# A graph network's segment sums on one core: when VectorE reads the table positions of the gathered groups

## The chip, the cores and the metric

The kernel runs on one core of a Trainium2 chip, as one launch. The metric is the device time of that launch in microseconds (us). A core has five engines that run their own instruction streams and meet at semaphores: TensorE (PE in the profile; PEld is its weight load), VectorE (DVE), ScalarE (ACT), GpSimd (POOL) and SyncE (SP), beside 16 DMA engines. Each engine has a sequencer that reads the stream in order, does register work and waits itself, and hands the rest to the engine. In the profile the sequencer's own instructions carry a q (DVEq).

## The reference, cut to what matters

Two layers of a graph network over 12500 nodes and 200000 edges, with the edges sorted by destination. The first layer is a pair of neighbour sums:

```python
agg = jax.ops.segment_sum(x[src], dst, num_segments=segments)   # 12500 x 32
h = relu(agg @ W_l_in.T + b_l_in + x @ W_r_in.T)
out = segment_sum(h[src], dst) @ W_l_out.T + b_l_out + h @ W_r_out.T
x = layernorm(x + out)
```

The second layer is an attention layer on the same edges (scores per edge, softmax over a destination's edges, a weighted segment sum, a projection and a layernorm). The change touches only the two neighbour sums of the first layer.

## The kernel before, in words

Each neighbour sum is one call of `segment_sum_pass`, the first with the tag sum_x, the second with the tag sum_y. In the trace the first lies between about 80 and 940 us, the second between about 980 and 1730 us. The rest of the span belongs to other functions. A pass adds the rows of the source nodes of 200000 sorted edges into a table in SBUF, `table_a`, which has the nodes along its free axis. It does so in two ways at once.

**The head** is the part of the edges with many edges per destination. It isn't gathered. VectorE makes, for tiles of 128 edges, two small 0/1 matrices: `lows` (line 1054) and `cells` (line 1066, written into the tile e_tab). TensorE multiplies them (line 981), which counts how often each source stands in each destination. ScalarE copies the counts to SBUF (line 949, one eviction for each unit of two PSUM banks). TensorE multiplies a block's counts with the node values (`parts`, line 1006). VectorE reduces the result and makes its places (lines 1090 and 1092), TensorE shifts it into a window of 128 nodes (line 1019), and VectorE adds the window into `table_a` at a position that is data (line 1104). That position is one number, read into a register by the load of line 1095, once for each block. In the first pass SyncE also stores the counts of 48 blocks to DRAM, 3200 KB each (line 901, count_scratch). In the second pass those blocks are loaded instead of counted.

**The tail** is gathered. GpSimd issues indirect DMAs (line 892) that bring 8 tiles of 128 edges for each slot; a slot is two groups of 512 edges, and four slots are in flight (SLOTS = 4). TensorE multiplies a group's rows with a 0/1 matrix (line 1030), made by VectorE in the first pass (`make_onehot`, line 1040) and by ScalarE in the second. VectorE adds the two windows of a slot into `table_a`: one addition for each group in the first pass, on 96 partitions, three in the second, on 32 partitions each (line 1123). The positions of the two groups are data too. They stand in `win`, an int32 row on partition 0 with one number for each group.

**Order.** Everything is written out by hand in steps: `Plan` assigns units, products, window additions and gathered tiles to steps by a table of costs, and each engine's program walks the same steps. VectorE's program makes the cells two steps ahead of their use (LEAD = 2) into a ring of four (RING = 4). In each step it makes cells, then reduces, then adds windows of the head, then makes the next 0/1 matrix of the tail, then adds the tail's windows. The additions of a slot stand one step after its last matrix product.

**The load.** Line 1112 reads positions of `win` into registers of VectorE's sequencer. It stands in front of the additions of every fourth slot, ahead of the wait for the slot's product, and reads the positions of four slots, eight numbers, with one instruction (six for the last three slots of the first pass). In the first pass the first slot is number 129, so the first load begins at number 258 of `win`; in the second it is slot 144, number 288.

```python
if i % SLOTS == 0:
    last = min(G, (n0 + i + SLOTS) * SG)
    starts = nc.values_load_multi_w_load_instructions(
        win[0:1, (n0 + i) * SG:last], engines=DVE_ENGINE, min_val=0, max_val=N,
        skip_runtime_bounds_check_because=CLAMPED)[1]
dve.wait_ge(summed, i + 1)
```

Of the kernel before, what the change touches and what calls it, by code (L numbers as in the profile page):

```python
# [23 lines left out]
DVE_ENGINE = [mybir.EngineType.DVE]  # L24
# [6 lines left out]
WINDOW = 128  # L31
SLOTS = 4
SG = 2
# [15 lines left out]
CLAMPED = "set-up clamps the starts"  # L49
# [206 lines left out]
def build(nc, x, src, dst, edge_attr, wl_in, bl_in, wr_in, wl_out, bl_out, wr_out,  # L256
          w1, b1, w2s, b2s, w2d, b2d, attn, out):
    N, E = x.shape[0], src.shape[0]
    IT, G, J, NCH = sizes(N, E)
# [20 lines left out]
    with ExitStack() as whole:  # L280
# [38 lines left out]
        table_a = sb("table_a", [P, NCH * GROUP])  # L319
# [6 lines left out]
        win = sb("win", [1, G], I32)  # L326
# [9 lines left out]
        at = COUNTS  # L336
        head_key, at = scratch[:, at:at + HT], at + HT
        head_low, at = scratch[:, at:at + HT], at + HT
        spare_at = at
        count_up, at = scratch[:, at:at + WIDEST * NK // 2].bitcast(F16), at + WIDEST * NK // 2  # L340
# [22 lines left out]
        with ExitStack() as ctx:  # L363
# [3 lines left out]
            even, last = FULLJ // 16 * 16, min(96, FULLJ // 32 * 32)  # L367
# [453 lines left out]
        def segment_sum_pass(tag, table_dram, values, plan, store):  # L821
# [14 lines left out]
            with ExitStack() as ctx:  # L836
# [199 lines left out]
                def _(dve):  # L1036
# [34 lines left out]
                    if not read:  # L1071
# [1 line left out]
                        dve.memset(unused[:, :, 56:], 0.0).then_inc(padded, 1)  # L1073
                        dve.tensor_copy(whole_row, iota[:, :]).then_inc(numbered, 1)
                        dve.wait_ge(numbered, 1)
                    made, starts, heads_added, tails_added = plan.first_item, [], 0, 0
                    if not lent:
                        make_onehot(0)
                    for step in range(plan.steps):
                        while made < plan.end_item and head.items[made]["first"] < (  # L1080
                                plan.first_unit + plan.made_by[step + LEAD]):
                            make_cells(made)
                            made += 1
                        for b in plan.parts_at.get(step, ()):
                            j = plan.place[b]
                            dve.wait_ge(multiplied, j + 1)
                            if j >= 2:
                                dve.wait_ge(windowed, j - 1)
                            columns = head.blocks[b]["columns"]
                            dve.tensor_scalar(places[0:columns, j % 2, :], iota[0:columns, :],  # L1090
                                              head_rel[0:columns, b:b + 1], UNPAIR, ALU.is_equal, ALU.mult)
                            dve.tensor_reduce(sums[0:columns, j % 2, :], product_of(j)[0:columns, :]  # L1092
                                              .rearrange("p (w f) -> p f w", w=3), AX.X, ALU.add).then_inc(summed_up, 1)
                        for b in plan.add_at.get(step, ()):
                            first = nc.values_load_multi_w_load_instructions(
                                head_win[0:1, b:b + 1], engines=DVE_ENGINE, min_val=0, max_val=N,
                                skip_runtime_bounds_check_because=CLAMPED)[1][0]
                            dve.wait_ge(windowed, plan.place[b] + 1)
                            if plan.place[b]:
                                dve.wait_ge(head_added, plan.place[b])  # L1100
                            if tails_added:
                                dve.wait_ge(tail_added, tails_added)
                            to = table_a[2 * F:3 * F, bass.ds(first, WINDOW)]
                            dve.tensor_tensor(to, to, window_of(plan.place[b]), ALU.add).then_inc(head_added, 1)
                            heads_added += 1
                        for i, t in taken.get(step, ()):
                            if t == 0 and lent <= i + 1 < slots:
                                make_onehot(i + 1)
                        for i in adds.get(step, ()):
                            if i % SLOTS == 0:  # L1110
                                last = min(G, (n0 + i + SLOTS) * SG)
                                starts = nc.values_load_multi_w_load_instructions(
                                    win[0:1, (n0 + i) * SG:last], engines=DVE_ENGINE, min_val=0, max_val=N,
                                    skip_runtime_bounds_check_because=CLAMPED)[1]
                            dve.wait_ge(summed, i + 1)
                            for g in range(SG):
                                for rows, sums_of in takes:
                                    if tails_added:
                                        dve.wait_ge(tail_added, tails_added)
                                    if heads_added:  # L1120
                                        dve.wait_ge(head_added, heads_added)
                                    to = table_a[rows, bass.ds(starts[i % SLOTS * SG + g], WINDOW)]
                                    dve.tensor_tensor(to, to, slot_sums(i, g)[sums_of, :], ALU.add)\
                                       .then_inc(tail_added, 1)
                                    tails_added += 1
# [1423 lines left out]
```

## Time and profile before

| what | value |
|---|---|
| median of 3 runs | 3997.3 us (3989.62 to 3998.96) |
| the profiled execution | 4001.15 us, its span 3999.3 us |
| PE busy over the span | 2838.4 us, 71% |
| DVE busy | 2714.7 us, 68% |
| ACT busy | 2490.8 us, 62% |
| POOL busy | 2638.2 us, 66% |

The span is the time from the first to the last instruction; 1.85 us of the profiled execution lie outside it. The shares are averages over stages with different limits, so they don't say what bounds a sum pass; that is read stage by stage. In a row that tells what ended an engine's idle time, a name after the arrow is the instruction that released it. "issue" means that the profile shows nothing that the engine waited for: its sequencer was busy with something else or hadn't got there yet.

### The profile page before, as it was taken

What the parts mean: (1) busy time and instruction counts of PE and PEld (TensorE: products, weight loads), DVE (VectorE), ACT (ScalarE), POOL (GpSimd) and SP (SyncE); (2) the same over time, 40 slices, a digit from 0 to 9 for tenths busy, and PEclk for the clock granted to TensorE, in tenths of its full rate; (3) what the DMA queues carried; (4) which work ended last, traced back from release to release, by engine and by line L of the source; (5) the groups of instructions that cost most, each with busy time, mean ns of one, the idle gap of its engine ahead of it and who ended that gap; (6) DMA issues with size and microseconds to landing.
All of it is one profiled execution on the core that took longest, in us unless ns stands there. A gap on an engine that the chain in (4) does not pass through costs nothing. (4 is left out here: it accounts for less than half of the span.)

```text
span 3999.3 us, 82215 instructions
## 1 busy us (share of the span) xinstructions
PE 2838.4 (71%) x28125; PEld 2379.6 (60%) x28125; DVE 2714.7 (68%) x7548; ACT 2490.8 (62%) x7102; POOL 2638.2 (66%) x2669
## 2 busy tenths in 40 slices
PE   3688788887888888874567666676666666667646
PEld 2566566664777777764456655565555665656644
DVE  7898766774455455562467777777876777777776
ACT  4566666775666566630167766787666776677745
POOL 3466765774655565427777777777777777777735
PEclk9999989998999999985567776677776777677767
DMA  3677875113666676723333333333333333333311
GB/s 88 237 284 312 315 313 213 21 20 118 223 232 234 222 237 222 237 92 69 76 77 87 90 85 76 87 94 86 85 82 78 93 87 83 79 82 88 89 31 39
DMA packets 285952, 536.14 MB, mean 134 GB/s; under 512 B 116631, under 2 KB 203217, under 8 KB 278902
## 3 DMA queue, kind: packets, MB, share of 16 engines
q1 hardware_dynamic: 200032, 452.07, 32.7%
q0 software_dynamic: 80256, 76.21, 10.2%
q8 instruction: 229, 3.75, 0.4%
q10 hardware_dynamic: 5246, 2.56, 0.2%
q14 instruction: 189, 1.55, 0.1%
HBM read 355.50 MB, written 175.09 MB: 133 GB/s over the span
## 5 line engine op out<-in xcount | busy, mean ns | idle before, releaser
L2034 POOL DMA_INDIRECT scratch<-fs_scratch,src_idx x728 | 728.8, 1001 | 222.0 <-issue 221.4
L892 POOL DMA_INDIRECT gath<-x_parts,src_idx x532 | 538.8, 1013 | 316.6 <-issue 191.5
L949 ACT ACTIVATE scratch<-sum_x_ps_c 128x600 int32<-128x600 f32 (+5 forms) x690 | 520.0, 770 | 311.2 <-PE sum_x_ps_c L981 266.6
L1066 DVE TENSOR_SCALAR e_tab<-scratch,e_tab 128x700 bf16<-128x700 f16 (+8 forms) x1380 | 526.1, 423 | 257.8 <-PE sum_y_ps_c L981 226.5
L892 POOL DMA_INDIRECT gath<-y_parts,src_idx x412 | 406.6, 987 | 291.6 <-issue 121.0
L2162 ACT ACTIVATE scratch<-scratch,bias,weight 128x32 f32<-128x32 f32 x1360 | 483.7, 399 | 77.2 <-DVE bias L2232 77.2
L2076 PEld LDWEIGHTS ps_e<-fdw,scratch 128*128 128x128 f32 x3136 | 494.3, 239 | 23.2
L2243 DVE SCALAR_TENSOR_TENSOR scratch<-ps_e,attn_sb 128x128 f32<-128x128 f32 x784 | 189.4, 284 | 429.0 <-PE ps_e L2076 427.8
L2076 PE MATMUL ps_e<-fdw,scratch 128*128 128x66 f32 x3136 | 478.0, 319 | 0.0
L949 ACT ACTIVATE scratch<-sum_y_ps_c 128x700 int32<-128x700 f32 (+2 forms) x348 | 280.1, 832 | 279.7 <-PE sum_y_ps_c L981 274.5
L1006 PEld LDWEIGHTS sum_x_ps_d<-parts,scratch 128*128 128x128 f16 x7400 | 383.3, 101 | 102.3 <-ACT scratch L949 44.4
L2142 ACT ACTIVATE scratch<-iota,dst_rel 128x128 f32<-128x128 f32 x824 | 251.2, 387 | 307.3 <-PE ps_m L2096 307.3
L1006 PE MATMUL sum_x_ps_d<-parts,scratch 128*128 128x96 bf16 x7400 | 419.0, 211 | 28.1 <-DVE scratch L1092 16.7
L981 PE MATMUL sum_x_ps_c<-e_tab,onehot 128*128 128x300 bf16 (+5 forms) x1380 | 323.3, 320 | 153.8 <-DVE e_tab L1066 116.2
L2034 POOL DMA_INDIRECT nodes<-fs_scratch,src_idx x332 | 325.7, 981 | 101.3 <-issue 100.9
L2034 POOL DMA_INDIRECT kept_spare<-fs_scratch,src_idx x280 | 274.4, 980 | 85.4 <-issue 85.1
L2096 PE MATMUL ps_m<-scratch 128*64 128x128 f32 x1456 | 266.6, 359 | 20.7 <-DVE scratch L2285 16.5
L2034 POOL DMA_INDIRECT gath<-fs_scratch,src_idx x224 | 225.3, 1006 | 76.4 <-issue 68.0
L1006 PE MATMUL sum_y_ps_d<-parts,scratch 128*128 128x96 bf16 x4500 | 239.8, 212 | 36.8 <-DMA scratch<-count_scratch 21.2
L2070 PE MATMUL ps_e<-scratch,ident 128*128 128x264 f32 x364 | 150.6, 553 | 155.5 <-DMA scratch<-fs_scratch,src_idx 155.4
L2096 PEld LDWEIGHTS ps_m<-scratch 128*64 128x64 f32 x1456 | 238.0, 188 | 31.1 <-DVE scratch L2285 18.1
L1006 PE MATMUL sum_y_ps_c<-parts,scratch 128*128 128x96 bf16 x4500 | 241.2, 213 | 18.9 <-ACT scratch L949 15.2
(363 smaller groups left out, 6241.3 us busy)
## 6 DMA issues: line engine op xcount, KB each, us to landing
count_scratch<-scratch SPq DMA_DIRECT2D x48, 3200.0 KB
scratch<-count_scratch SPq DMA_DIRECT2D x192, 800.0 KB
onehot<-rel_scratch SPq DMA_DIRECT2D x196, 256.0 KB
scratch<-in_edge_attr_2x SPq DMA_DIRECT2D x390, 128.0 KB
fdw<-fd_scratch SPq DMA_DIRECT2D x392, 33.0 KB
scratch<-fs_scratch,src_idx POOLq DMA_INDIRECT x728
gath<-x_parts,src_idx POOLq DMA_INDIRECT x532
gath<-y_parts,src_idx POOLq DMA_INDIRECT x412
```

Source lines behind the costliest of these rows:

```text
L892: pool.indirect_dma_start(out=rows_in(s, t), out_offset=None, in_=table_dram, in_offset=bass.IndirectOffsetOnAxis(ap=src_idx[:, g, k:k + 1 ...
L949: act.activation(to, ps_c[u % pairs][:, :, 0:q].rearrange("p h (d a) -> p h a d", d=d), ACT.Copy).then_inc(kept, 1)
L981: m = pe.matmul(ps_c[u % pairs][:, h, 0:q], lows[:, tile // LOWS % RING, tile % LOWS, :], cells[:, item % RING, at:at + q], start=True, st ...
L1006: m = pe.matmul(product_of(j), counts[:, plan.buffer(b), a, :], parts[:, a, :], start=(a == 0), stop=(a == NK - 1))
L1066: d = dve.tensor_scalar(cells[:, n % RING, i * width:(i + 1) * width], count_up[:, 0:width], head_key[:, tile:tile + 1], head_weight[:, ti ...
L2034: pool.indirect_dma_start(out=rows_of(m)[:, t, :], out_offset=None, in_=fs_dram, in_offset=bass.IndirectOffsetOnAxis(ap=src_idx[:, g, k:k ...
L2070: pe.matmul(ps_e[s % 2][g][:, :, 0:ROW], ident[:, :], rows_of(m)[:, g * K:(g + 1) * K, :], start=True, stop=False)
L2076: t = pe.matmul(ps_e[s % 2][g][:, k, 0:ROW], oht[:, s % 2, g * K + k, :], fdw[:, s, g, :], start=False, stop=(k == K - 1))
L2096: t = pe.matmul(ps_m[par][:, g * WINDOW:(g + 1) * WINDOW], rows_of(n - 2)[:, g * K + k, 0:HID], oh_msg[:, par, g * K + k, :], start=(k == ...
L2142: far = act.activation(to[:, t, :], iota[:, :], ACT.Square, bias=places[:, t:t + 1], scale=-1.0)
L2162: e = act.activation(rows, rows, ACT.Exp, bias=bias[:, q, i:i + 1], scale=weight[:, q, i:i + 1], accum_out=total[:, q, i:i + 1] if i < K * ...
L2243: dve.scalar_tensor_tensor(parts[:, :, h, 0:F], ps_e[s % 2][g][:, :, h * F:(h + 1) * F], 0.0, wide(attn_sb[:, h * F:(h + 1) * F], 1, [P, K ...
```

## The change

The block that loaded eight positions in every fourth slot goes. In its place stand, in every slot, two loads of one position each, for the slot's two groups, at the same place of the program: behind the previous work of VectorE and ahead of the wait for the slot's product. The additions take their position from these two. Nothing else changes.

```diff
-                    made, starts, heads_added, tails_added = plan.first_item, [], 0, 0
+                    made, heads_added, tails_added = plan.first_item, 0, 0
...
                         for i in adds.get(step, ()):
-                            if i % SLOTS == 0:
-                                last = min(G, (n0 + i + SLOTS) * SG)
-                                starts = nc.values_load_multi_w_load_instructions(
-                                    win[0:1, (n0 + i) * SG:last], engines=DVE_ENGINE, min_val=0, max_val=N,
-                                    skip_runtime_bounds_check_because=CLAMPED)[1]
+                            at = (n0 + i) * SG
+                            starts = [nc.values_load_multi_w_load_instructions(
+                                win[0:1, at + g:at + g + 1], engines=DVE_ENGINE, min_val=0, max_val=N,
+                                skip_runtime_bounds_check_because=CLAMPED)[1][0] for g in range(SG)]
                             dve.wait_ge(summed, i + 1)
...
-                                    to = table_a[rows, bass.ds(starts[i % SLOTS * SG + g], WINDOW)]
+                                    to = table_a[rows, bass.ds(starts[g], WINDOW)]
```

Where the instructions go is plainest in VectorE's own stream. In the rows below ISA is a register operation of the sequencer that waits and forms the address of the addition behind it; lines below the removed one are numbered one lower in the changed kernel. The first place is a slot of the first pass that had the eight-value load, the first slot of the pass:

```order
 L1104 ISA
 L1104 TENSOR_TENSOR table_a<-table_a,sum_x_ps_c 32x128
-L1112 TENSOR_LOAD win
-L1123 ISA
-L1123 TENSOR_TENSOR table_a<-table_a,sum_x_ps_s 96x128
-L1123 ISA
-L1123 TENSOR_TENSOR table_a<-table_a,sum_x_ps_s 96x128
+L1111 TENSOR_LOAD win x2
+L1122 ISA
+L1122 TENSOR_TENSOR table_a<-table_a,sum_x_ps_s 96x128
+L1122 ISA
+L1122 TENSOR_TENSOR table_a<-table_a,sum_x_ps_s 96x128
```

One load instruction of eight numbers has become two of one number, at the same spot.

The second place is the slot after it on VectorE, one of the three in four that had no load. Its additions stand between the cells of line 1066:

```order
 L1054 TENSOR_TENSOR onehot<-sum_x_ps_c,scratch 128x512
 L1066 TENSOR_SCALAR e_tab<-scratch,e_tab 128x200 x2
-L1123 ISA
-L1123 TENSOR_TENSOR table_a<-table_a,sum_x_ps_c 96x128
-L1123 ISA
-L1123 TENSOR_TENSOR table_a<-table_a,sum_x_ps_c 96x128
+L1111 TENSOR_LOAD win x2
+L1122 ISA
+L1122 TENSOR_TENSOR table_a<-table_a,sum_x_ps_c 96x128
+L1122 ISA
+L1122 TENSOR_TENSOR table_a<-table_a,sum_x_ps_c 96x128
```

Two loads now stand in front of additions that had none.

The third place is such a slot of the second pass, on VectorE, right behind the reduction of a head block:

```order
 L1090 TENSOR_SCALAR scratch<-iota,head_rel 126x128
 L1092 TENSOR_REDUCE scratch<-sum_y_ps_d 126x32
-L1123 ISA
-L1123 TENSOR_TENSOR table_a<-table_a,sum_y_ps_c 32x128 x3
-L1123 ISA
-L1123 TENSOR_TENSOR table_a<-table_a,sum_y_ps_c 32x128 x3
+L1111 TENSOR_LOAD win x2
+L1122 ISA
+L1122 TENSOR_TENSOR table_a<-table_a,sum_y_ps_c 32x128 x3
+L1122 ISA
+L1122 TENSOR_TENSOR table_a<-table_a,sum_y_ps_c 32x128 x3
```

Here too two loads are new, behind two short instructions. The streams of the other four engines hold the same instructions in the same order.

## Rows read from the trace of the kernel before

**Rows 1.** Stretches: busy PE, PEld, DVE, ACT, POOL, then clock, DMA share, GB/s
```profile
130.00:300.00 170.00, 127.34 (x1737) 100.58 (x1738) 149.84 (x434) 101.25 (x147) 98.86 (x97) 0.90 0.68 266
300.00:690.00 390.00, 314.06 (x4372) 236.81 (x4372) 277.69 (x705) 240.56 (x286) 254.08 (x250) 0.93 0.76 295
690.00:940.00 250.00, 219.65 (x3224) 168.13 (x3225) 173.96 (x418) 176.73 (x221) 155.39 (x155) 0.98 0.10 17
990.00:1730.00 740.00, 620.80 (x10233) 522.36 (x10230) 369.43 (x1009) 450.59 (x805) 400.28 (x405) 0.93 0.66 223
```

**Rows 2.** The eight-value load, line 1112: 345:352, 690:900, 900:940, 990:1700 us; min/median/max
```profile
L1112 DVEq TENSOR_LOAD <-win x1: 6942/6942/6942, 345.3 to 345.3; - x1
...
L1112 DVEq TENSOR_LOAD <-win x5: 1848/1849/1853, 695.6 to 867.8; - x5
...
L1112 DVEq TENSOR_LOAD <-win x1: 1409/1409/1409, 906.9 to 906.9; - x1
...
L1112 DVEq TENSOR_LOAD <-win x13: 606/608/624, 1017.8 to 1678.5; - x13
```

**Rows 3.** The one-value load, line 1095: 110:690 and 990:1730 us
```profile
L1095 DVEq TENSOR_LOAD <-head_win x48: 300/310/1049, 114.2 to 678.3; - x48
...
L1095 DVEq TENSOR_LOAD <-head_win x90: 299/308/325, 992.4 to 1723.8; - x90
```

**Rows 4.** All engines and DMA while the load at 345.3 ran
```profile
345.30:352.30 7.00, 3.29 (x59) 2.80 (x57) 1.46 (x2) 2.89 (x4) 5.19 (x6) 0.89 1.03 412
```

**Rows 5.** VectorE around the load that began at 345.3, timeline
```profile
345.57 1.23 DVE L1040 TENSOR_TENSOR onehot<-sum_x_ps_c,dst_rel 128x1024 bf16<-128x1024 f32 x1
352.51 0.70 DVE L1123 TENSOR_TENSOR table_a<-table_a,sum_x_ps_s 96x128 f32 x2 [5.72 <-issue]
```

**Rows 6.** What VectorE waited for: stretches 130:300, 300:690, 690:940
```profile
DVE table_a L1123 <- issue: 14.3, 3, 6.0
...
DVE table_a L1123 <- issue: 33.5, 8, 6.9
...
DVE table_a L1123 <- issue: 5.6, 6, 1.7
```

**Rows 7.** The same view around three single loads: 298:301, 443:447, 541:545
```profile
DVE table_a L1123 <- issue: 1.4, 1, 1.4
...
DVE table_a L1123 <- issue: 1.2, 1, 1.2
...
DVE table_a L1123 <- issue: 2.7, 1, 2.7
```

**Rows 8.** ScalarE's evictions of counts, line 949, per stretch; (x) is their number
```profile
321.30:345.30 24.00, 13.53 (x17) 0.93 0.80 309
345.30:357.30 12.00, 3.73 (x5) 0.73 0.69 259
357.30:381.30 24.00, 15.43 (x19) 0.99 0.73 288
```

**Rows 9.** What TensorE waited for: stretches 130:690 and 990:1730
```profile
PE sum_x_ps_c L981 <- DVE e_tab L1066: 74.6, 55, 7.1
...
PE sum_y_ps_c L981 <- DVE e_tab L1066: 3.4, 3, 2.4
```

**Rows 10.** Additions at line 1123: stretches 130:300 and 300:690, and the whole span
```profile
L1123 DVE TENSOR_TENSOR table_a<-table_a,sum_x_ps_s x12: 271/284/285, 138.2 to 276.0; 96x128 f32 x12
...
L1123 DVE TENSOR_TENSOR table_a<-table_a,sum_x_ps_s x32: 270/284/286, 300.6 to 671.2; 96x128 f32 x32
...
L1123 DVE TENSOR_TENSOR table_a<-table_a,sum_y_ps_s x156: 278/282/289, 1018.7 to 1710.5; 32x128 f32 x156
```

**Rows 11.** VectorE around one addition of the second pass, timeline
```profile
1058.34 0.25 DVE L1092 TENSOR_REDUCE scratch<-sum_y_ps_d 126x32 f32<-126x96 f32 x1
1058.62 1.98 DVE L1123 TENSOR_TENSOR table_a<-table_a,sum_y_ps_c 32x128 f32 x6
```

**Rows 12.** ScalarE's wait for the stores of counts, stretch 300:690
```profile
ACT scratch L949 <- DMA count_scratch<-scratch: 23.8, 18, 2.9
```

## The prediction

> **What bounds the kernel now.** I first read the busy time of the engines by stretch [rows 1], because the change touches only the two sum passes. From 130 to 300 us VectorE is the fullest engine (149.84 of 170 us, 88%). From 300 to 690 it is busy for 277.69 of 390 us and TensorE for 314.06; from 690 to 940 TensorE has 219.65 of 250 us. In the second pass VectorE is busy for half of the time (369.43 of 740 us) and TensorE for 84%. So what VectorE loses should count in full in the first stretch, in part in the second, and hardly at all later.
>
> Then the load itself. In the quiet last part of the first pass eight numbers take 1.849 us and six take 1.409 us [rows 2]: 0.220 us for each number and 0.089 us around them. The one-value load of line 1095 has a median of 0.310 us [rows 3], which is 0.089 + 0.220. While a store of counts is under way the same eight-value load takes up to 6.942 us [rows 2], with the DMA engines full (share 1.03, 412 GB/s) [rows 4]: 0.857 us for each number. In the second pass eight numbers take only 0.608 us [rows 2], though the DMA share is 0.66 there too [rows 1]; those transfers write SBUF and the stores read it, and the load also begins at another place of `win`. I can't tell here which of the two makes it cheap.
>
> Next, who pays. The sequencer runs ahead of the engine, so part of a load lies beside work already handed over. The load at 345.3 us began while line 1040 still had until 346.80 us to run, a lead of 1.5 us, and the addition came 0.25 us behind the load's end, after 5.72 us of idle time [rows 2, 5]. From 690 us on, five loads of 1.85 and one of 1.41 us are 10.65 us; with 0.25 us behind each that is 12.15 us, of which 5.6 us show as idle [rows 6]. The mean lead is (12.15 - 5.6) / 6 = 1.1 us.
>
> Last, what such an idle stretch costs the pass. ScalarE evicts one unit of counts after another. It made 17 and 19 evictions in the 24 us on either side of the load at 345.3 us, 0.75 in a us, and 5 in the 12 us from its start [rows 8]. Nine were due, so 4 / 0.75 = 5.3 us were lost, of the 5.72 us that VectorE idled. A long stall passes through almost whole. TensorE's wait for the cells of line 1066 says the same: 74.6 us in the first pass, up to 7.1 us at a time [rows 9].
>
> **Removed: the eight-value load.** VectorE idled for it 14.3 us in 3 places before 300 us and 33.5 us in 8 places up to 690 us [rows 6]. Three of these are short (1.4, 1.2 and 2.7 us) [rows 7]; I count them at nothing, since a stall of that length can be taken up by the two steps that the cells are made ahead. The eight long ones are 14.3 + 33.5 - 5.3 = 42.5 us, and I count them whole. The 5.6 us after 690 us count nothing either, as TensorE is 88% busy there and VectorE has 30% to spare. **Gain: 42.5 us.** At the other end it is 47.8 us, with the short ones.
>
> **Added in the first pass: two one-value loads in each slot.** There are 12 slots up to 300 us and 32 from there to 690 us (a slot has two additions, and the _c rows number as many as the _s rows) [rows 10]. Away from a store the pair takes 2 x 0.31 + 0.25 = 0.87 us, under the lead of 1.1 us, and is hidden by line 1040 or by the cells in front; without that cover it would cost the 0.87 us. Under a store the slowest eight-value load makes it 0.089 + 0.857 = 0.95 us for one number, and the slowest of the 48 one-value loads took 1.049 us [rows 3]; as not every load meets a full queue from end to end, I take 0.9 us. The pair leaves 1.8 + 0.25 - 1.1 = 0.95 us uncovered. The trace has no two loads in a row. If they overlapped, 0.9 + 0.25 - 1.1 = 0.05 us would remain; one after the other at 1.05 us each, behind a lead of only 0.25 us (one short instruction, as in [rows 11]), it would be 2.1 us. I take 0.95 us, since each further number in one load also adds its full price. Stores are under way for most of this time (DMA share 0.68 and 0.76) [rows 1] and hit 8 of the 11 loads hard, so I take four slots in five: 10 and 26.
> - Up to 300 us: 10 x 0.95 = **9.5 us**, counted whole.
> - From 300 to 690 us: 26 x 0.95 = 24.7 us of idle time in small pieces, of which I count a third, **8 us**. TensorE often waits for cells, so not nothing, but the short stalls look cheap.
> - After 690 us: 23 pairs, hidden.
>
> **Added in the second pass.** 312 additions, six for each slot, make 52 slots [rows 10]. Many stand right behind lines 1090 and 1092, with no idle time today [rows 11]; that is some 0.5 us of lead, so 0.87 - 0.5 = 0.4 us shows, about 20 us of VectorE's idle time in all. TensorE waited for cells there only 3.4 us in 3 places [rows 9], so I count a tenth: **2 us**.
>
> Behind the waiting sequencer stand the cells of the next units, for which TensorE waits. The additions also free the PSUM window of the slot after next, which has a slot's time to spare.
>
> **Sum:** 42.5 - 9.5 - 8 - 2 = 23 us. The profiled execution took 4001.15 us (its span 3999.3), so it would take 3978 us; the median of the runs is 3.85 us lower, which makes 3997.3 - 23 = **3974 us**.
>
> **A rule that speaks against the change.** The price of one value is 0.299 us at least and 0.308 us in the median of 90 loads [rows 3]. The Trainium skill, page "DMA: Bandwidth & Descriptors", section "Latency and other measured facts", gives a `tensor_load` a floor of about 600 ns, and says that compilers unroll by four to spread it. By that rule the trace disagrees, at 0.308 us; the rival below shows what a floor would do. The page "Runtime: NRT & Kernel Launch", section "Instruction fetch mechanics", has about 200 ns for each register even in bulk: the quiet first pass agrees (220 ns), the second does not (608 / 8 = 76 ns).
>
> **The rivals.**
> - *The lead swallows the pairs.* If the small waits are all taken up, or the two loads overlap, the gain is the whole 42.5 us, or 47.8 us with the short stalls: 3955 to 3950 us. For it: the stall of 2.7 us looks cheap. Against: VectorE has 12% to spare up to 300 us. Chance 0.2.
> - *Every small wait counts.* TensorE's 74.6 us of waits for cells in 55 places [rows 9] show a chain with little play. Then 36 x 0.95 + 2 = 36 us are lost and 6 us gained: 3991 us. Chance 0.12.
> - *The stores bind.* ScalarE already waits 23.8 us in 18 places for the stores of counts [rows 12], and stores run on while VectorE stalls. If half of the 28.2 us removed after 300 us only turn into that wait, the gain is 9 us: 3988 us. Chance 0.07.
> - *Slower: the pairs under a store are bare.* With 1.05 us for each load and the short lead, 36 slots x 2.1 us = 76 us against 42.5 us: 33 us slower, 4031 us. It decides from 42.5 / 36 = 1.2 us of uncovered time for each slot. For it: slots where no line 1040 stands in front; against: the mean lead of 1.1 us. Chance 0.1.
> - *A floor for each load instruction.* Here each load would cost at least the 0.606 us of the cheapest eight-value one [rows 2]. A quiet pair then takes 1.46 us, uncovered by 0.4 us in the first pass and by 1 us in the second; a third of 52 us and of 31 x 0.4 us would be given back, 21 us in all: 3995 us. This is the rule of the page named above. Chance 0.03.
> - That the change doesn't do what it says is excluded by the order of VectorE's instructions, which shows the two loads in every slot.
>
> **How the numbers follow.** My own case has 0.48, with a range of its own from 3960 to 3985 us. The range for 8 times in 10 runs from the first rival's end, 3950 us, to 3995 us; outside are the slower rival and a little of the others. About 0.3%, 12 us, is what a measurement can tell from no change: faster means below 3985 us. Faster: 0.48 + 0.2 = 0.68; the same: 0.12 + 0.07 + 0.03 = 0.22; slower: 0.1.
>
> **What would show it.** Right: no load of line 1111 above 1.1 us; no idle time before an addition longer than about 2 us in the first pass; VectorE's idle time before the additions up to 690 us near 35 us instead of 47.8; the first pass shorter by some 25 us, the second by nothing or longer by 2; in the second pass about 20 us of "issue" before the additions. Wrong: single loads well above 1 us under a store, TensorE's waits for cells not falling from 74.6 us, or ScalarE's wait for stores growing by as much as they fall.

## The result, and the profile after

| kernel | median, us | ratio to before, 95% interval |
|---|---|---|
| before | 3993.46 (3985.73 to 3998.96, 4 runs) | |
| changed | 3953.55 (3945.08 to 3957.59, 4 runs) | 0.9902 (0.9882 to 0.9921) |

The change makes the kernel faster by 39.9 us, 1.0%. The forecast was a gain of 23 us and a time of 3974 us. The direction was right and the time lies in the stated range, but the gain is 1.7 times the one predicted. (The 3974 us were reckoned from 3997.3 us, the median of the first three runs of the kernel before; from 3993.46 us they are 19.5 us away, half of what came.) The profiled execution of the changed kernel is the fastest of its four (3945.08 us), so its span overstates the gain; the comparison below goes by the length of the two passes in the two profiled executions.

The length of a pass can be read from ScalarE's evictions of counts. In the rows, the two times behind the durations are the first and the last start. Before:

```profile
L949 ACT ACTIVATE scratch<-sum_x_ps_c x690: 504/760/1134, 79.4 to 928.3; 128x600 int32<-128x600 f32 x50, 128x700 int32<-128x700 f32 x45, 128x800 int32<-128x800 f32 x30, 128x400 int32<-128x400 f32 x20
...
L949 ACT ACTIVATE scratch<-sum_y_ps_c x348: 733/837/1021, 985.8 to 1715.3; 128x700 int32<-128x700 f32 x90, 128x800 int32<-128x800 f32 x56, 128x900 int32<-128x900 f32 x28
```

and after:

```profile
L949 ACT ACTIVATE scratch<-sum_x_ps_c x690: 503/760/1132, 80.0 to 880.5; 128x600 int32<-128x600 f32 x50, 128x700 int32<-128x700 f32 x45, 128x800 int32<-128x800 f32 x30, 128x400 int32<-128x400 f32 x20
...
L949 ACT ACTIVATE scratch<-sum_y_ps_c x348: 731/837/1021, 936.9 to 1665.4; 128x700 int32<-128x700 f32 x90, 128x800 int32<-128x800 f32 x56, 128x900 int32<-128x900 f32 x28
```

The first pass went from 928.3 - 79.4 = 848.9 us to 880.5 - 80.0 = 800.5 us, 48.4 us shorter. The second stayed (729.5 and 728.5 us). The spans differ by 56.1 us; the 6.7 us outside the two passes lie in code that the change doesn't touch, and I take them for scatter. So the gain lies in the first pass.

The loads of the changed kernel, by stretch (min/median/max in ns), the answer to [rows 2]:

```profile
L1111 DVEq TENSOR_LOAD <-win x96: 299/906/1046, 132.0 to 684.5; - x96
...
L1111 DVEq TENSOR_LOAD <-win x38: 301/303/314, 694.9 to 876.7; - x38
...
L1111 DVEq TENSOR_LOAD <-win x104: 299/308/321, 970.5 to 1671.2; - x104
```

A one-value load takes 0.30 us quiet, in both passes, and 0.91 us in the median of the stretch with the stores; none is longer than 1.05 us. That is as forecast (0.31, 0.9 and 1.1 us). What VectorE waited for in front of the additions, in the stretches 130:300, 300:690, 690:870 and 935:1740, the answer to [rows 6]:

```profile
DVE table_a L1122 <- issue: 3.7, 8, 1.3
...
DVE table_a L1122 <- issue: 14.1, 17, 1.8
...
DVE table_a L1122 <- issue: 0.4, 1, 0.4
...
DVE table_a L1122 <- issue: 4.7, 15, 0.7
```

The idle time up to 690 us fell from 47.8 to 17.8 us (35 were forecast), and after it from 5.6 to 0.4 us. In the second pass there are 4.7 us, where about 20 were forecast. The busy time by stretch, as in [rows 1], and TensorE's wait for the cells, as in [rows 9]:

```profile
130.00:300.00 170.00, 134.82 (x1871) 107.11 (x1871) 160.69 (x467) 108.60 (x157) 106.98 (x105) 0.93 0.73 287
...
300.00:690.00 390.00, 334.41 (x4789) 253.44 (x4788) 298.82 (x750) 264.48 (x317) 287.51 (x274) 0.97 0.75 288
...
990.00:1730.00 740.00, 619.97 (x9736) 525.91 (x9733) 389.46 (x1130) 442.63 (x935) 384.54 (x397) 0.94 0.64 214
```

```profile
PE sum_x_ps_c L981 <- DVE e_tab L1066: 46.2, 52, 2.3
```

VectorE is now busy for 160.69 of 170 us up to 300 us, against 149.84. The granted clock of TensorE rose too, from 0.90 to 0.93 and from 0.93 to 0.97 in the first two stretches. TensorE's wait for cells fell from 74.6 to 46.2 us. The stores of counts took a little back: ScalarE waited for them 31.2 us from 300 to 690 us, against 23.8 [rows 12] (26 to 31 us in the four profiles of kernels with pairs in the whole first pass):

```profile
ACT scratch L949 <- DMA count_scratch<-scratch: 31.2, 21, 2.8
```

### The profile page after: what moved, and what is told of

Same layout as the page of the kernel before. It is cut to its first block and busy times, and to the rows that moved or that the text cites. A ratio compares the mean times of both kernels' runs of the same rounds, so it can differ in the third digit from the quotient of the medians.

```text
span 3943.2 us, 82423 instructions
## 1 busy us (share of the span) xinstructions
PE 2831.0 (72%) x28125; PEld 2379.0 (60%) x28125; DVE 2713.9 (69%) x7548; ACT 2489.6 (63%) x7102; POOL 2640.4 (67%) x2669
## 5 line engine op out<-in xcount | busy, mean ns | idle before, releaser
L2033 POOL DMA_INDIRECT scratch<-fs_scratch,src_idx x728 | 718.0, 986 | 221.9 <-issue 221.6
L892 POOL DMA_INDIRECT gath<-x_parts,src_idx x532 | 549.9, 1034 | 262.8 <-issue 193.8
L2075 PEld LDWEIGHTS ps_e<-fdw,scratch 128*128 128x128 f32 x3136 | 502.3, 243 | 22.8
L2075 PE MATMUL ps_e<-fdw,scratch 128*128 128x66 f32 x3136 | 486.1, 323 | 0.0
L1006 PEld LDWEIGHTS sum_y_ps_d<-parts,scratch 128*128 128x128 f16 x4500 | 220.1, 102 | 53.2 <-DMA scratch<-count_scratch 23.4
```

The lines of the kernel that those rows point to most:

```text
L892: pool.indirect_dma_start(out=rows_in(s, t), out_offset=None, in_=table_dram, in_offset=bass.IndirectOffsetOnAxis(ap=src_idx[:, g, k:k + 1 ...
L1006: m = pe.matmul(product_of(j), counts[:, plan.buffer(b), a, :], parts[:, a, :], start=(a == 0), stop=(a == NK - 1))
L2033: pool.indirect_dma_start(out=rows_of(m)[:, t, :], out_offset=None, in_=fs_dram, in_offset=bass.IndirectOffsetOnAxis(ap=src_idx[:, g, k:k ...
L2075: t = pe.matmul(ps_e[s % 2][g][:, k, 0:ROW], oht[:, s % 2, g * K + k, :], fdw[:, s, g, :], start=False, stop=(k == K - 1))
```

## Experiments

Ratios are to the kernel before, run beside each kernel on the same chip. The lengths of passes come from one profiled execution each, by the evictions as above. In the edits, which are cut, load(...) stands for the long call that fills one register for each number of its slice. `store` is true in the first pass alone, `at` is the slot's first number in `win`, G the length of that row, and IG is eight, the positions of four slots.

| kernel | median, us | ratio (interval) | first pass, us | second pass, us |
|---|---|---|---|---|
| before | | | 848.9 | 729.5 |
| changed | 3953.55 | 0.9902 (0.9882 to 0.9921) | 800.5 | 728.5 |
| x_pairs_only | 3953.11 | 0.9894 (0.9868 to 0.9919) | 801.6 | 732.1 |
| one_load_per_pass | 3938.65 | 0.9846 (0.9827 to 0.9865) | 790.2 | 731.9 |
| pairs_twice_x | 3952.72 | 0.9884 (0.9865 to 0.9903) | 801.8 | 730.3 |
| four_in_one_x | 4002.05 | 1.0018 (1.0003 to 1.0033) | 852.2 | 732.5 |
| pairs_until_690 | 3947.82, 1 run | | 807.2 | 732.5 |
| quarter_stores | 3945.27 | 0.9872 (0.9854 to 0.9890) | 798.8 | 724.4 |
| aligned_eight | 3948.26 | 0.9868 (0.9844 to 0.9891) | 794.0 | 731.0 |
| swapped_alignment | 3951.64, 1 run | | 805.8 | 729.9 |
| aligned_four | 3937.35 | 0.9849 (0.9826 to 0.9872) | 794.1 | 726.9 |
| changed_again | 3950.82 | 0.9879 (0.9860 to 0.9898) | 806.2 | 726.6 |
| aligned_four_again | 3944.07 | 0.9851 (0.9830 to 0.9871) | 792.8 | 733.3 |

Four kernels have the pairs in the whole first pass (changed, x_pairs_only, pairs_twice_x as it turned out, changed_again): 800.5 to 806.2 us, and ratios from 0.9879 to 0.9902, a gain of 39 to 48 us. The two with aligned eights there differ by 11.8 us. So one profile tells lengths apart only to some 6 us, or 12 at worst.

### The second pass: x_pairs_only

```diff
-    starts = [load(win[0:1, at + g:at + g + 1]) for g in range(SG)]
+    if store:     # the first pass
+        starts, begun = [load(win[0:1, at + g:at + g + 1]) for g in range(SG)], at
+    elif i % SLOTS == 0:
+        begun, starts = at, load(win[0:1, at:min(G, at + IG)])
```

> The first pass has the changed kernel's two one-value loads in each slot, the second pass the eight-value load of before in every fourth slot. Theory (the whole gain is the end of the long stalls of the first pass): as fast as the changed kernel within 3 us, so about 40 us under the kernel before; the first pass lasts 801 us as in the changed kernel, the second 729 to 731 us. Rival (the pairs cost something in the second pass, as the prediction had it with 2 us, or up to 20 us if every uncovered piece counts): faster than the changed kernel by 2 to 20 us, with a second pass of 710 to 728 us.

Its median is 0.4 us from the changed kernel's, and the second pass with eights is 732.1 us long, with pairs 726.6 to 730.3 us. The pairs cost nothing there that could be seen, though VectorE idles 4.7 us for them. The 2 us that the prediction took off for the second pass don't show, within a scatter of that pass from 726.6 to 733.3 us among kernels that run it at all alike.

### All loads together: one_load_per_pass

```diff
-    starts = [load(win[0:1, at + g:at + g + 1]) for g in range(SG)]
+    if i == 0:
+        starts = load(win[0:1, at:at + SG])
```

> The positions of the first slot of a pass are loaded once and used for all of its slots, so the windows of the tail go to a wrong place; 117 of the 119 pairs of loads are gone and nothing else. It measures what all loads of the additions cost together. Theory (the pairs are hidden by the sequencer's lead, and the small uncovered pieces are taken up): 0 to 6 us faster than the changed kernel. Rival (each uncovered piece counts, 17.8 us before 690 us and 5.9 us in the second pass): 18 to 24 us faster than the changed kernel, about 60 us under before.

This is the floor: the evictions of the first pass, and TensorE's wait for the cells.

```profile
L949 ACT ACTIVATE scratch<-sum_x_ps_c x690: 504/762/1140, 79.9 to 870.1; 128x600 int32<-128x600 f32 x50, 128x700 int32<-128x700 f32 x45, 128x800 int32<-128x800 f32 x30, 128x400 int32<-128x400 f32 x20
...
PE sum_x_ps_c L981 <- DVE e_tab L1066: 32.9, 46, 2.2
```

The first pass lasts 790.2 us. Against it the kernel before lost 848.9 - 790.2 = 58.7 us to its eights and the changed one 10.3 us to its pairs (10 to 16 us over the four executions). Two profiles further below idle as little before the additions (aligned_four and aligned_four_again, 1.2 and 1.5 us up to 690 us) and last 794.1 and 792.8 us, so the floor is known to some 4 us: against them the eights cost 55 to 56 us and the pairs 6 to 13. By the medians the eights cost 1.5% of 4001 us, 62 us (54 to 69), and the pairs some 14 us (pairs_twice_x, which ran beside this kernel, is 14.1 us slower). Both numbers for the pairs are larger than my theory of "nearly free" allowed (0 to 6 us) and smaller than the rival (18 to 24 us). The truth is between: 18.2 us of uncovered time before the additions of the first pass (3.7 + 14.1 + 0.4) cost 10 to 16 us. The floor isn't free of other waits. ScalarE waits longest for the stores of counts here, 42.9 us from 130 to 690 us, against 32.9 in the changed kernel and 28.7 in the kernel before:

```profile
ACT scratch L949 <- DMA count_scratch<-scratch: 42.9, 27, 2.9
```

That may be why part of the pairs' idle time isn't lost; no run separates it.

### A repeat that was meant to double the loads: pairs_twice_x

```diff
+    for again in range(2 if store else 1):
         starts = [load(win[0:1, at + g:at + g + 1]) for g in range(SG)]
```

> As the changed kernel, but in the first pass each pair of one-value loads is issued twice, four loads in a slot; the second reading is used. Under a store a slot's loads then take 4 x 0.91 + 0.15 = 3.8 us, and with 0.25 us behind them and a lead of 1.5 us leave 2.5 us idle in some 36 slots, 90 us; quiet ones take 1.3 us and leave 0.5 us in some 31 slots, 16 us. Theory (short pieces are taken up, longer ones pass through whole): in the changed kernel the pairs are nearly free, and here 50 to 100 us are lost against it, so the kernel is slower than before by 10 to 60 us. Rival (anything below some 3 us is taken up by the cells made ahead): less than 25 us lost against the changed kernel.

The trace has 96 loads up to 690 us, as many as the changed kernel:

```profile
L1112 DVEq TENSOR_LOAD <-win x96: 299/918/1066, 130.8 to 684.7; - x96
```

The first reading of each pair has no user, and it isn't in the program that ran. So this tells nothing of doubled loads, and serves as a second measurement of the changed kernel: 0.9884.

### Twice the numbers in each slot: four_in_one_x

```diff
-    starts = [load(win[0:1, at + g:at + g + 1]) for g in range(SG)]
+    begun = min(at - 1, G - 4) if store else at
+    starts = load(win[0:1, begun:begun + (4 if store else SG)])
```

> In the first pass one load in each slot reads four numbers from an odd place of win (one before the slot's two, the two, and one behind), in the second one load of two. It doubles the numbers read in each slot of the first pass. Four numbers should take 0.97 us quiet and 3.5 us under a store; with 0.25 us behind and a mean lead of 1.5 us that leaves about 2.2 us idle in each of some 36 slots, 80 us. Theory (idle time beyond what the lead covers is lost nearly whole): the first pass lasts 860 to 880 us, against 800.5 in the changed kernel, and the kernel is slower than before. Rival (stalls of up to 3 us are taken up by the cells made ahead): the first pass lasts less than 825 us.

Loads up to 690 us, VectorE's idle time before the additions, and the busy time and clock from 130 to 690 us:

```profile
L1112 DVEq TENSOR_LOAD <-win x43: 968/3377/3627, 131.9 to 678.8; - x43
...
DVE table_a L1123 <- issue: 69.4, 37, 3.4
...
130.00:690.00 560.00, 439.14 (x5986) 335.12 (x5986) 422.00 (x1128) 336.26 (x424) 359.34 (x343) 0.92 0.74 286
```

Four numbers take up to 3.63 us under a store, as worked out. The longest stall is 3.4 us, and there are 37 of them. Had stalls of this length been taken up, as I had assumed for three of the eights, the first pass would have stayed under 825 us. It lasts 852.2 us, 62 us over the floor, for 69.4 + 1.5 = 70.9 us of idle time (1.5 after 690 us): 87% of it is lost. The pass is some 8 us shorter than I expected, and the kernel is again as slow as the one before. The last load of the pass is the only one that begins at a multiple of four (388), and it takes 0.36 us where the quiet ones beside it take 0.97.

### Late eights: pairs_until_690

```diff
-    starts = [load(win[0:1, at + g:at + g + 1]) for g in range(SG)]
+    if store and i < 44:
+        starts, begun = [load(win[0:1, at + g:at + g + 1]) for g in range(SG)], at
+    elif i % SLOTS == 0:
+        begun, starts = at, load(win[0:1, at:min(G, at + IG)])
```

> The first pass has the changed kernel's pairs in its first 44 slots, while the stores run, and the eight-value load of before in every fourth slot after them; the second pass has eights. Theory (late in the pass each uncovered piece of 0.4 to 1.7 us in front of the additions is lost too, although VectorE is only 70% busy): the last 23 slots take 6 to 8 us longer than in the changed kernel, as in the kernel before, and the first pass lasts 806 to 808 us. Rival (the prediction's step, which counted those 5.6 us at nothing; the kernel before lost its 7 us there to something else): the first pass lasts 800 to 802 us.

The eights of the quiet stretch, and the idle time in front of the additions there:

```profile
L1117 DVEq TENSOR_LOAD <-win x5: 1406/1847/1861, 697.3 to 864.9; - x5
...
DVE table_a L1128 <- issue: 4.7, 5, 1.6
```

Each trace has the start times of the same 690 evictions, so the lag of a kernel behind one_load_per_pass can be followed through the first pass. In us, counted from each kernel's first eviction:

| eviction (its time in the kernel before) | 60 (127) | 180 (267) | 330 (504) | 480 (691) | 689 (928) |
|---|---|---|---|---|---|
| before | 0.1 | 15.4 | 33.4 | 51.3 | 58.7 |
| changed | 0.1 | 2.2 | 6.4 | 9.5 | 10.3 |
| pairs_until_690 | 0.2 | 2.8 | 5.9 | 12.4 | 16.9 |
| four_in_one_x | 0.2 | 19.0 | 37.3 | 59.1 | 62.0 |

Behind the 480th eviction the kernel before lost 7.4 us for 5.6 us of idle time, pairs_until_690 4.5 us for 5.6 us (the sixth late eight, at 656.5 us, left 0.9 us beside the 4.7 above), and quarter_stores, the kernel of the next section, with the same late eights, 7.6 us for 5.6 us. The kernels without unaligned eights there lost 0.6 to 2.9 us. So late stalls of under 2 us do cost most of their length, where VectorE is busy for only 70% of the time. The step of the prediction that counted them at nothing falls. The expectation isn't met in full: the last slots took 3.7 us longer than in the changed kernel, not 6 to 8, and the 807.2 us lie in its bounds by luck, since 2.9 us of the lag came before the 480th eviction, where the two kernels are alike. It is also a single run.

The same starts show the price of each eight of the kernel before, up to 690 us. The last row is the growth of its lag behind one_load_per_pass, from the mean of the 10 us ahead of the load to the mean from 9 to at most 25 us behind its start; between the loads the lag moves by up to 1.3 us by itself, and the floor has 1.2 us of idle time of its own at its one load, at 132 us.

| load at, us | 131 | 194 | 248 | 298 | 345 | 395 | 444 | 489 | 540 | 586 | 641 |
|---|---|---|---|---|---|---|---|---|---|---|---|
| VectorE idle, us | 6.0 | 5.3 | 2.9 | 1.4 | 5.7 | 4.9 | 1.2 | 5.8 | 2.7 | 4.9 | 6.9 |
| lag grows by, us | 4.7 | 6.1 | 4.4 | 1.4 | 6.5 | 4.9 | 0.6 | 6.1 | 2.4 | 5.5 | 8.3 |

The eight long stalls cost 46.5 us for 42.5 us of idle time, the three short ones (298, 444 and 540 us) 4.4 us for 5.3 us. A single short step is no larger than the drift, but the short ones together aren't nothing.

### Is it the stores? quarter_stores

```diff
-    sp.dma_start(count_dram[b, :, :], counts[:, b % 2, :, :].rearrange("p a q -> p (a q)"))
+    sp.dma_start(count_dram[b, :, 0:NK * P // 4],
+                 counts[:, b % 2, 0:NK // 4, :].rearrange("p a q -> p (a q)"))
...
-                 count_dram[b, :, rows.start * P:rows.stop * P])
+                 count_dram[b, :, 0:NK * P // 4])
```

> The kernel before, with its eight-value loads, but each of the 48 stores of counts of the first pass writes only its first quarter, 800 KB in place of 3200, and the second pass loads that quarter four times, so the counts of three quarters of the rows are replaced there. Theory (a number that isn't read as part of an aligned block costs 0.22 us alone and 0.86 us while a store reads SBUF): most loads of the first pass now take 1.85 us, those that meet a store for its 2.5 us up to 4; the idle time before the additions falls from 47.8 us to 12 to 20 us up to 690 us, and the first pass lasts 805 to 820 us against 848.9 us. Rival (the loads are slowed by the gathers or by GpSimd, which start at the same moment as the additions): the loads still take up to 6.9 us, and the first pass lasts over 830 us.

The eights up to 690 us, the idle time before the additions, and the busy time from 300 to 690 us with the DMA share in the column before the last:

```profile
L1113 DVEq TENSOR_LOAD <-win x13: 1847/1852/2774, 132.1 to 686.8; - x13
...
DVE table_a L1124 <- issue: 12.7, 12, 2.8
...
300.00:690.00 390.00, 335.39 (x4878) 255.29 (x4876) 302.30 (x756) 270.50 (x323) 285.25 (x278) 0.98 0.29 86
```

With the stores cut to a quarter and the gathers as they were, the slowest eight-value load takes 2.77 us and the median is the quiet 1.85 us. The stores are what slows the loads; the gathers and GpSimd, busy as before, don't. The idle time, 12.7 us, is as expected. The pass is shorter than my 805 to 820 us, and isn't the eights' cost alone, since ScalarE no longer waits for stores either.

### What makes the second pass's eights cheap: aligned_eight and swapped_alignment

```diff
-    starts = [load(win[0:1, at + g:at + g + 1]) for g in range(SG)]
+    if i == 0 or at % IG == 0:          # in swapped_alignment at % IG == SG in the second pass
+        begun, starts = at, load(win[0:1, at:min(G, (at // IG + 1) * IG)])
```

> Loads of eight positions as before, but each begins at a multiple of eight numbers of the row win: the first pass reads six numbers at 258 and then eight from 264 on; the second pass is as before. Theory (a load that begins at a multiple of eight numbers is read as one block, others number by number): the quiet loads of the first pass take 0.61 us as in the second pass, not 1.85 us; under a store at most 1.3 us for all eight, not 6.9. Then the first pass is as short as the changed kernel's or up to 5 us shorter, about 40 to 45 us under before. Rival (what makes the second pass's load cheap is that nothing reads SBUF by DMA there): the loads keep 1.85 us quiet and up to 6.9 us under a store, and the time is that of before within 8 us.

> Loads of eight positions; in the first pass they begin at multiples of eight numbers of win, in the second two numbers behind such a multiple (so six numbers first and then eight). Theory (the place in the row decides): the quiet loads of the second pass now take 1.85 us, as the first pass's did in the kernel before, although nothing there reads SBUF by DMA; none takes over 2.1 us, as its DMA traffic writes SBUF and one-value loads stayed at 0.31 us under it. The second pass lasts 729 to 735 us, as VectorE waits for TensorE there anyway. Rival (the kind of DMA traffic decides): they stay at 0.61 us.

Loads of aligned_eight up to 690 us and after:

```profile
L1113 DVEq TENSOR_LOAD <-win x13: 607/1833/5031, 130.9 to 675.2; - x13
...
L1113 DVEq TENSOR_LOAD <-win x4: 608/610/612, 715.8 to 842.5; - x4
```

Loads of swapped_alignment in the second pass, and what VectorE waited for there at "issue":

```profile
L1113 DVEq TENSOR_LOAD <-win x14: 535/1852/1879, 975.5 to 1649.9; - x14
...
DVE table_a L1124 <- issue: 16.0, 12, 1.8
```

An eight-value load that begins at a multiple of eight numbers takes 0.61 us quiet, in the first pass too. One that begins two numbers behind it takes 1.85 us in the second pass too. So the place in the row decides, and the DMA traffic of the second pass, which writes SBUF, doesn't matter (1.88 us at most). (swapped_alignment's first load there reads two numbers, not the six of the expectation, and takes 0.535 us; its last reads six, in 1.41 us.) aligned_eight's first pass, 794.0 us, is 6.5 us shorter than the changed kernel's. Under a store the aligned eight takes 1.8 us, up to 1.9, rather than the 1.3 us that I had as a bound; only the first load, six numbers from 258 on, still takes 5.03 us. swapped_alignment, a single run, leaves 16 us of idle time in the second pass, and that pass is 729.9 us long as ever: uncovered time on VectorE costs nothing there that could be seen.

### The better version: aligned_four

```diff
-    starts = [load(win[0:1, at + g:at + g + 1]) for g in range(SG)]
+    if i == 0 or at % 4 == 0:
+        begun, starts = at, load(win[0:1, at:min(G, (at // 4 + 1) * 4)])
```

> Loads of four positions, each at a multiple of four numbers of win, in every second slot, in both passes (the first slot of the first pass reads two). In the kernel with aligned loads of eight a quiet one took 0.61 us and one under a store some 1.85 us, about twice a one-value load. Theory (SBUF is read in blocks of four numbers, and each block costs one trip): four aligned numbers take 0.3 to 0.45 us quiet and 0.9 to 1.0 us under a store, which lies wholly within the sequencer's lead of 1.4 to 1.7 us in most slots; the first pass then lasts 790 to 793 us against 800.5 us in the changed kernel, and the kernel is 7 to 10 us faster than the changed one. Rival (a block is eight numbers, and the doubled time under a store has another cause): a load of four takes as long as one of eight, 0.6 and 1.85 us, there are twice as many of them, and the first pass lasts 797 us or more.

Loads up to 690 us and after, the idle time before the additions up to 690 us, and TensorE's wait for the cells:

```profile
L1113 DVEq TENSOR_LOAD <-win x25: 343/960/1706, 131.2 to 675.2; - x25
...
L1113 DVEq TENSOR_LOAD <-win x9: 342/347/351, 696.9 to 861.2; - x9
...
DVE table_a L1124 <- issue: 1.2, 1, 1.2
...
PE sum_x_ps_c L981 <- DVE e_tab L1066: 30.8, 41, 2.2
```

Four aligned numbers take 0.35 us quiet and 0.96 us under a store, hardly more than one, as the theory of blocks of four has it. It needs a limit: a load that begins elsewhere pays for each number, also where it takes in a whole block (the eight numbers from 346 hold 348 to 351 and take 1.85 us quiet), and two numbers from a multiple of eight take 0.53 us. The loads' own times speak against the rival; the first pass, 794.1 us, is 1 us over the expected bounds and under the rival's 797, but by less than the scatter. By the ratios the kernel is 12 to 21 us faster than those with pairs, more than the 7 to 10 us expected. One slow load is left, the first with its two numbers, and 1.2 us of idle time. The second measurement stands beside one of the changed kernel:

> The changed kernel once more, beside the kernel with aligned loads of four on the same chip. Theory (the uncovered pieces of the pairs cost some 10 us in the first pass and nothing in the second): a ratio to the kernel before of 0.988 to 0.991, a first pass of 799 to 803 us.

> Aligned loads of four once more, on the same chip as the changed kernel. Theory: 8 to 16 us faster than the changed kernel, a ratio to the kernel before of 0.984 to 0.987, a first pass of 790 to 796 us. Rival (the two aligned kernels differ between executions by as much as the 12 us seen between the two kernels with aligned eights, and the gain over the changed kernel was chance): less than 4 us between the two.

The first pass lasts 792.8 us and is within the expected bounds. The changed kernel's, 806.2 us, is above its bounds, by the scatter told above; its ratio, 0.9879, is just outside the expected 0.988 to 0.991. Aligned fours are 6.8 us faster by the medians and 11 us by the ratios. That is a little short of the 8 us expected, by the medians. The intervals of the two ratios overlap, but each of the five runs with aligned fours (3933.9 to 3946.76 us) is faster than each of the five of the changed kernel (3948.2 to 3955.45 us). This version beats both kernels.

## Why the prediction was right in direction and short in size

Against the floor of one_load_per_pass, by the prediction's own terms:

| term | predicted, us | shown, us |
|---|---|---|
| eights removed | 42.5 | 58.7 (first pass; 54 to 69 by the medians, both passes) |
| pairs, first pass | -17.5 | -10.3 (-10 to -16) |
| pairs, second pass | -2 | 0 |
| sum | 23 | 48 in the profiled pass, 40 by the medians |

**The step that failed is the price of the removed loads**, the 42.5 us, for which the runs showed 58.7 us. I counted the eight long stalls whole and gave three short ones (5.3 us) and the late ones (5.6 us) the value nothing, since cells are made two steps ahead and VectorE has time to spare there. By the steps of the lag in the kernel before, the short ones cost 4.4 us, the late stretch 7.4 us, and the long ones 46.5 us: 58.3 us. So 11.8 us of the 16.2 missing are what I had put at nothing, and some 4 us are the long stalls, which cost a little more than VectorE's idle time. With 10.9 us of idle time added, my own term would have been 53.4 us. Why VectorE's spare time doesn't take up a stall is argued, not shown: from 130 to 690 us VectorE waits for TensorE too (31.3 us in front of line 1104 alone, in the rows of the kernel before), while TensorE waits for its cells, so its idle time lies in other places than the stall and may not be there to draw on.

```profile
DVE table_a L1104 <- PE sum_x_ps_c L1019: 31.3, 22, 2.7
```

Whether the clock has a part in the last 4 us stays open. From 130 to 690 us TensorE's granted clock was 0.92 on average in the kernel before and 0.96 in the changed one. With levels of 1.2 and 2.4 GHz, a mean of 0.92 is 0.16 of 560 us at the lower level, 90 us, and 0.96 is 45 us. In the 12 us from the start of the load at 345 us it was 0.73 [rows 8]. The two kernels with aligned eights have the same loads in the first pass and 9.9 and 10.2 us of idle time for them up to 690 us, yet last 794.0 us at a mean clock of 0.97 and 805.8 us at 0.94, so clock and length go together there although the loads are alike. Against it: four_in_one_x also had 0.92 and lost less than its idle time. No run separates the clock, and 4 us are within the scatter of the profiles.

**The pairs were over-priced by their lead.** Their own durations were right: 0.30 and 0.91 us, one after the other, not overlapped. What was wrong is the work in front of them. I took the lead of the eights, 1.1 us, for all slots. The order shown ahead of the prediction had a better case in its second place, a slot with line 1054 and two cells in front of the additions. In the changed kernel such a pair, and VectorE around it, look so:

```profile
L1111 DVEq TENSOR_LOAD <-win x2: 893/904/914, 148.5 to 149.4; - x2
```

```profile
148.82 0.29 DVE L1104 TENSOR_TENSOR table_a<-table_a,sum_x_ps_c 32x128 f32 x1
149.14 0.69 DVE L1054 TENSOR_TENSOR onehot<-sum_x_ps_c,scratch 128x512 bf16<-128x512 f32 x1
149.75 0.57 DVE L1066 TENSOR_SCALAR e_tab<-scratch,e_tab 128x200 bf16<-128x200 f16 x2
150.53 0.70 DVE L1122 TENSOR_TENSOR table_a<-table_a,sum_x_ps_c 96x128 f32 x2 [0.21 <-issue]
```

The pair begins at 148.5 us and VectorE has work until 149.75 + 0.57 = 150.32 us, a lead of 1.9 us, so 2 x 0.91 + 0.25 us leave 0.21 us bare. Not every slot is like it: by the timeline, the 37 pairs up to 690 us that took 1.5 us or more had leads from 0.3 to 2.2 us, 1.4 us on average. I predicted 34 us of idle time up to 690 us and there were 17.8 that the profile puts down to the loads; in some slots the addition had to wait for TensorE's product all the same. Of that idle time I counted half (17.5 of 34), and 10 to 16 of 18.2 us were lost, so the share was set too low here as well, and the two errors partly cancel.

**The rivals.** That the lead swallows the pairs has part of the truth, but with a cost left of 10 to 16 us; that the measured 3953.55 us stands beside its 3955 is chance, a removed term 16 us too small against pairs counted at nothing. That every small wait counts, to which I gave 0.12, names the mechanism that the runs showed in the first pass; its 3991 us were far off, since it had 34 us of small waits where there were 18, and still left out the short stalls of the eights. The stores took back only 2 to 7 us of waiting. The slower case needed 1.2 us of uncovered time in each slot; it was 0.4 us over the 44 slots. On the rule that a register load has a floor of about 600 ns (the Trainium skill, "DMA: Bandwidth & Descriptors", "Latency and other measured facts"): 104 loads in the second pass have a median of 0.308 us and a minimum of 0.299 us, so the trace disagrees. The price of about 200 ns for each register even in bulk (the Trainium skill, "Runtime: NRT & Kernel Launch", "Instruction fetch mechanics"), told there of the runtime's own loads from HBM, where these read SBUF, agrees with unaligned loads (four 0.97 us, eight 1.85 us) and disagrees with aligned ones, where four cost 0.35 us together.

## What to carry to other kernels

A register load that waits for nothing can still be the longest stall of a stage: look for "issue" in front of an instruction with a data-dependent address, and for the load's duration on the sequencer's row, stretch by stretch. Take an uncovered stall at close to its full length where two engines wait for each other in turn, even when they look 20 and 30% idle; that holds for the short stalls too. And before splitting a load, see where it begins: aligned groups of four numbers took nearly the time of one here.

## What the runs showed of the hardware

- A load into VectorE's registers from an SBUF row: one number 0.30 us, two 0.53 us (at every even place, a multiple of eight too); four from an odd place 0.97 us, eight from two behind a multiple of eight 1.85 us; four from a multiple of four 0.35 us, eight from a multiple of eight 0.61 us. Other places weren't tried.
- While DMA reads SBUF at about 410 GB/s: one number 0.91 us, four aligned 0.96 us, eight aligned 1.8 us, four unaligned up to 3.6 us, eight unaligned up to 6.9 us. These fit a trip for each number, or for each four in a load that begins at a multiple of four; the trips themselves are in no trace. DMA that writes SBUF (share 0.64 to 0.66) changed nothing: one number took 0.325 us at most.
- Two one-value loads in a row don't overlap: a pair took 0.65 us quiet and 1.8 to 2.0 us under a store.
